# Narrow products in pairs over opposite halves of the rows, packed mixing weights, four mixture buffers and another unit order, in the recurrent block of a five-layer kernel

## What is computed

```python
xa = ln(x); sx = previous_token(xa) - xa
xxx = tanh((xa + sx * maa_x) @ maa_w1)            # 512 -> 5 x 32
xxx = einsum('blfd,fde->blfe', xxx, maa_w2)       # each 32 -> 512
xk, xw, xv, xr, xg = xa + sx * (maa_stack + xxx)
w = exp(-exp(time_decay + tanh(xw @ td_w1) @ td_w2))   # 512 -> 64 -> 512
r, k, v, g = xr @ Wr.T, xk @ Wk.T, xv @ Wv.T, silu(xg @ Wg.T)
# 32 heads of 16 x 16 state: out_t = r_t (u * k_t v_t + s), s = k_t v_t + w_t * s
x1 = x + groupnorm(out) * g @ Wo.T
x2 = x1 + sigmoid(xr2 @ Wfr.T) * (relu(xk2 @ Wfk.T) ** 2 @ Wfv.T)   # on ln(x1)
```

## Time and profile before

| what | value |
|---|---|
| median of 3 runs | 3742.41 us (3740.49 to 3743.94) |
| the profiled execution's own time | 3743.95 us |
| its span, first to last instruction | 3742.2 us |
| PE busy over the span | 3455.5 us (92%) |
| DVE, POOL, ACT busy | 2347.7, 2015.8, 1833.4 us |
| mean granted TensorE clock | 0.967 |

### The profile page before, as it was taken

The page is one execution under the profiler, slowest core; times in us unless marked ns, Lnnn a source line. Parts: engine busy times, 40 slices in busy tenths (PEclk is TensorE's granted clock), DMA queues, the critical chain, the costliest instruction groups (busy, mean ns, idle before and its releaser), DMA issues. The chain is left out here.

```text
span 3742.2 us, 59765 instructions
## 1 busy us (share of the span) xinstructions
PE 3455.5 (92%) x23516; PEld 2672.5 (71%) x23516; DVE 2347.7 (63%) x2908; ACT 1833.4 (49%) x4242; POOL 2015.8 (54%) x1079
## 2 busy tenths in 40 slices
...
GB/s 146 90 127 46 81 57 58 58 70 69 46 59 75 51 49 55 72 67 30 30 74 52 46 41 49 93 23 12 23 147 6 13 18 1 18 18 18 12 18 12
DMA packets 114303, 189.92 MB, mean 51 GB/s; under 512 B 17904, under 2 KB 36848, under 8 KB 113392
## 3 DMA queue, kind: packets, MB, share of 16 engines
...
## 5 line engine op out<-in xcount | busy, mean ns | idle before, releaser
L1025 POOL TENSOR_TENSOR l_pr<-l_pr,l_inv 128x1024 f32<-128x1024 f32 x256 | 480.0, 1895 | 382.8 <-DVE l_inv L1087 382.8
L895 ACT ACTIVATE l_pr<-l_ps_s,l_top 128x512 f32<-128x512 f32 x512 | 348.6, 690 | 352.4 <-DVE l_top L1083 271.6
L1529 POOL TENSOR_TENSOR tok_pr<-tok_pr,tok_ma 128x1024 f32<-128x1024 f32 x128 | 304.1, 2399 | 283.1 <-DVE tok_pr L1907 283.1
L2774 POOL TENSOR_TENSOR rec_rs<-rec_sE,rec_rT 128x1024 f32<-128x1024 f32 x128 | 326.8, 2555 | 215.7 <-DVE rec_sE L3262 166.7
L1020 POOL TENSOR_TENSOR l_x_lo<-ahead_piece,l_x_hi 128x1024 fp32r<-128x1024 f32 (+1 forms) x97 | 294.1, 3032 | 154.1 <-ACT l_x_hi L879 154.1
L1083 DVE TENSOR_REDUCE l_top<-l_ps_s 128x2 f32<-128x1024 f32 x256 | 304.1, 1218 | 10.5 <-PE l_ps_s L669 10.5
L3262 DVE TENSOR_TENSOR_SCAN rec_sE<-rec_wE,rec_ps_v 128x1024 f32<-128x1024 f32 x128 | 292.7, 2286 | 5.5 <-POOL rec_rs L2774 1.1
L679 PE MATMUL l_ps_t<-l_ident,l_pr 128*128 128x128 f32 x2048 | 275.2, 277 | 11.0 <-POOL l_pr L1025 4.9
L679 PEld LDWEIGHTS l_ps_t<-l_ident,l_pr 128*128 128x128 f32 x2048 | 225.6, 141 | 78.2 <-issue 60.7
L1779 ACT ACTIVATE tok_pr<-tok_pr,tok_shift 128x256 f32<-128x256 f32 x512 | 253.7, 498 | 13.4 <-DVE tok_shift L1915 12.0
L630 PE MATMUL l_ps_b<-l_x_hi,l_w_lo 128*128 128x256 f32 x784 | 226.8, 289 | 0.0
...
## 6 DMA issues: line engine op xcount, KB each, us to landing
...
```

Of the source, the lines that this page charges most:

```text
L895: act.activation(pr[t][:, h, :], ps_s[:, t % 2, h, :], ACT.Exp, bias=top[:, t, h:h + 1], accum_out=mass[:, t, h:h + 1]).then_inc(exped, 1)
L1025: pool.tensor_tensor(pr[t][:, :, :], pr[t][:, :, :], inv[:, t, :].unsqueeze(2).to_broadcast([P, 2, FEAT]), ALU.mult).then_inc(scaled, 1)
L1529: pool.tensor_tensor(tile, tile, ma[u][:, :, :].rearrange("p t k -> p (t k)").unsqueeze(1).to_broadcast([P, 2, TT * TOK]), ALU.add).then_i ...
L2774: pool.tensor_tensor(rs[j % 2][:, :, :], sE[j % 2][:, :, :], rT[s][:, :, :], ALU.mult).then_inc(rs_made, 1)
```

## The change

Four things. First, the second mixing products and the decay's second product are issued in pairs, `Mw` with `Mk`, `Mv` with `Mr`, `Mg` with `D2` (`few_rows`): each contracts over 64 rows, the one over rows 0 to 63 and the other over rows 64 to 127, into the two banks. `XX1` writes 32 and `D1` 64 output partitions. Second, the weights are packed: `m1` 256 to 160 columns, `m2` 4 to 2 blocks, `t1` 128 to 64 columns, `t2_m2b` 2 blocks to 1. Third, there are four mixture buffers for two. Fourth, all schedules but the last pass's are new, and `place` counts units in PE's own order. `lay_out` fills the packed arrays (not shown); the waits on `mixtures` and `products` are the same but for the order w, k, v, r, g in every batch.

```diff
-
-
-    FIRST_UNITS = ("T0", "T1", "XX0", "XX1", "Mw0", "Mw1", "Mk0", "Mk1", "D1", "K0", "Mv0", "Mv1", "D20", "D21", "K1",
-                   "V0", "Mr0", "Mr1", "V1", "Mg0", "Mg1", "R0", "R1", "G0", "G1", "C")
-    A_UNITS = ("T0", "T1", "XX0", "XX1", "Mw0", "Mw1", "Mk0", "Mk1", "D1", "K0", "Mr0", "Mr1", "D20", "D21", "K1",
-               "R0", "Mg0", "Mg1", "R1", "Mv0", "Mv1", "G0", "G1", "V0", "V1", "C")
+    A_UNITS = ("T0", "T1", "XX0", "XX1", "D1", "K0", "K1", "R0", "R1", "G0", "G1", "V0", "V1", "C")
+
+    PAIRS = {"Mwk": ("Mw", "Mk"), "Mvr": ("Mv", "Mr"), "Mgd": ("Mg", "D2")}
+    NARROW_UNITS = tuple(n + h for pair in PAIRS.values() for n in pair for h in "01")
     Z_UNITS = ("E", "Q", "O0", "O1", "T0", "T1", "FK0", "FK1", "FR0", "FR1", "FV0", "FV1")
-    NA, NZ = len(A_UNITS), len(Z_UNITS)
-    PROLOGUE = "LS LN T0 T1 SX XX0 XX1 Mw0 Mw1 Mk0 Mk1 D1 K0 Mv0 Mv1 D20 D21 K1 V0 Mr0 Mr1 V1"
+    NA, NZ = len(A_UNITS + NARROW_UNITS), len(Z_UNITS)
+    PROLOGUE = "LS LN T0 T1 SX XX0 XX1 Mwk0 Mw0 Mk0 Mwk1 Mw1 Mk1 D1 Mvr0 Mv0 Mr0 Mvr1 Mv1 Mr1 K0 K1 Mgd0 Mg0 D20 Mgd1 Mg1 D21 V0 V1"
     FIRST_TENSOR_SCHEDULE = (
-        "L:Mg0 L:Mg1 L:R0 L:R1", "L:G0", "L:G1 L:C", "A:T0 A:T1", "", "A:XX0 A:XX1", "A:Mw0 A:Mw1 A:Mk0 A:Mk1",
-        "A:D1 A:K0", "A:Mr0 A:Mr1 A:D20 A:D21", "A:K1 A:R0", "A:Mg0 A:Mg1 A:R1", "A:Mv0 A:Mv1 A:G0", "A:G1 A:V0",
-        "A:V1 A:C B:T0 B:T1", "B:XX0 B:XX1", "B:Mw0 B:Mw1 B:Mk0 B:Mk1")
+        "L:R0 L:R1", "A:T0 A:T1", "L:C L:G0", "A:XX0 A:XX1", "L:G1", "A:Mwk0 A:Mwk1", "A:D1 A:Mvr0", "A:K0 A:Mvr1", "A:K1",
+        "A:R0", "A:R1 A:Mgd0", "A:V0 A:Mgd1", "A:V1", "A:G0 B:T0 B:T1", "A:C A:G1 B:XX0 B:XX1", "B:Mwk0 B:Mwk1")
     TENSOR_SCHEDULE = (
-        "A:D1 A:K0", "Z:E A:Mr0 A:Mr1 A:D20 A:D21", "Z:Q A:K1", "A:R0", "A:Mg0 A:Mg1 A:R1", "A:Mv0 A:Mv1", "Z:O0 A:G0",
-        "Z:O1 A:G1", "A:V0", "A:V1 Z:T0", "Z:T1 A:C B:T0 B:T1", "Z:FK0", "Z:FK1 B:XX0 B:XX1", "Z:FR0 B:Mw0 B:Mw1 Z:FR1",
-        "B:Mk0 B:Mk1 Z:FV0", "Z:FV1")
+        "A:D1 A:Mvr0", "Z:E A:Mvr1", "Z:Q A:K0", "A:K1 A:Mgd0", "A:R0", "Z:O0 A:Mgd1", "Z:O1 A:R1", "A:V0", "A:V1",
+        "A:G0 Z:T0 Z:T1", "A:C B:T0 B:T1 A:G1", "Z:FK0", "Z:FK1 B:XX0 B:XX1", "Z:FR0 B:Mwk0", "Z:FR1 B:Mwk1 Z:FV0",
+        "Z:FV1")
     FIRST_SCALAR_SCHEDULE = (
-        "L:Mg0 L:Mg1 L:R0 L:R1", "L:G0", "A:LN L:G1", "A:T0 A:T1", "", "A:XX0 A:XX1", "A:Mw0 A:Mw1 A:Mk0 A:Mk1",
-        "A:D1 A:K0", "A:Mr0 A:Mr1 A:D20 A:D21", "A:K1 A:R0", "A:Mg0 A:Mg1 A:R1", "A:Mv0 A:Mv1 A:G0", "B:LN A:G1 A:V0",
-        "A:V1 B:T0 B:T1", "B:XX0 B:XX1", "B:Mw0 B:Mw1 B:Mk0 B:Mk1")
+        "L:R0 L:R1", "A:LN A:T0 A:T1", "L:G0", "A:XX0 A:XX1", "L:G1", "A:Mw0 A:Mk0 A:Mw1 A:Mk1", "A:D1 A:Mv0 A:Mr0",
+        "A:K0 A:Mv1 A:Mr1", "A:K1", "A:R0", "B:LN A:R1 A:Mg0 A:D20", "A:V0 A:Mg1 A:D21", "A:V1", "A:G0 B:T0 B:T1",
+        "A:G1 B:XX0 B:XX1", "B:Mw0 B:Mk0 B:Mw1 B:Mk1")
     SCALAR_SCHEDULE = (
-        "A:D1 A:K0", "Z:E A:Mr0 A:Mr1 A:D20 A:D21", "Z:Q A:K1", "B:LN A:R0", "A:Mg0 A:Mg1 Z:N2 A:R1", "A:Mv0 A:Mv1",
-        "Z:O0 A:G0", "Z:O1 A:G1", "A:V0", "Z:LN A:V1 Z:T0", "Z:T1 B:T0 B:T1", "Z:FK0 Z:XA", "Z:FK1 B:XX0 B:XX1",
-        "Z:FR0 B:Mw0 B:Mw1 Z:FR1", "B:Mk0 B:Mk1", "")
+        "A:D1 A:Mv0 A:Mr0", "Z:E A:Mv1 A:Mr1", "Z:Q A:K0", "A:K1 A:Mg0 A:D20", "Z:N2 A:R0 B:LN", "Z:O0 A:Mg1 A:D21",
+        "Z:O1 A:R1", "A:V0", "A:V1", "Z:LN A:G0 Z:T0 Z:T1", "B:T0 B:T1 A:G1", "Z:XA Z:FK0", "Z:FK1 B:XX0 B:XX1",
+        "Z:FR0 B:Mw0 B:Mk0", "Z:FR1 B:Mw1 B:Mk1", "")
     FIRST_GPSIMD_SCHEDULE = (
-        "L:Mg1 L:RK", "A:LS", "", "", "A:SX", "", "A:Mw1", "A:Mk1", "", "A:Mr1", "B:LS", "A:Mg1", "A:Mv1", "A:RK", "B:SX",
+        "A:LS L:RK", "", "A:SX", "", "", "", "A:Mw1 A:Mk1", "A:Mv1", "A:Mr1", "B:LS", "", "", "A:Mg1 A:RK", "", "B:SX",
         "B:Mw1 B:Mk1")
     GPSIMD_SCHEDULE = (
-        "", "", "A:Mr1 B:LS", "Z:N1", "A:Mg1", "", "Z:O0 A:Mv1", "A:RK Z:O1", "Z:LS", "", "Z:X", "B:SX Z:XR", "", "Z:FK1",
-        "B:Mw1", "B:Mk1 Z:FV0 Z:FV1")
+        "", "", "A:Mv1", "Z:N1 A:Mr1", "B:LS", "Z:O0", "Z:O1", "A:Mg1 Z:LS", "A:RK", "", "Z:X", "B:SX Z:XR", "", "Z:FK1",
+        "", "B:Mw1 B:Mk1 Z:FV0 Z:FV1")
     FIRST_VECTOR_SCHEDULE = (
-        "L:Mg1", "A:LS", "", "L:G0 L:G1 L:C", "A:SX", "", "A:Mw1", "A:Mk1", "", "A:Mr1", "B:LS", "A:Mg1", "A:G0 A:Mv1",
-        "A:G1 A:V0", "A:V1 A:C B:SX", "B:Mw1 B:Mk1")
+        "A:LS", "", "", "A:SX L:C L:G0", "L:G1", "", "A:Mw1 A:Mk1", "A:Mv1", "A:Mr1", "B:LS", "", "", "A:V0 A:Mg1", "A:V1",
+        "A:G0 A:C A:G1 B:SX", "B:Mw1 B:Mk1")
     VECTOR_SCHEDULE = (
-        "", "Z:E", "A:Mr1 B:LS", "Z:I", "A:Mg1", "Z:N3", "A:Mv1", "A:G0", "Z:LS A:G1", "A:V0", "A:V1 A:C", "Z:X", "B:SX",
-        "", "B:Mw1", "B:Mk1 Z:FV0 Z:FV1")
+        "", "Z:E", "A:Mv1", "Z:I A:Mr1", "Z:N3 B:LS", "", "A:Mg1", "Z:LS", "A:V0 A:V1", "A:G0", "A:C Z:X", "A:G1", "B:SX",
+        "", "", "B:Mw1 B:Mk1 Z:FV0 Z:FV1")
...
-        m1, m2 = sb("m1", [P, FT, 2 * P]), sb("m2", [P, 4, FEAT])
-        t1, t2_m2b = sb("t1", [P, FT, P]), sb("t2_m2b", [P, 2, FEAT])
+        m1, m2 = sb("m1", [P, FT, P + MIX]), sb("m2", [P, 2, FEAT])
+        t1, t2_m2b = sb("t1", [P, FT, DECAY]), sb("t2_m2b", [P, FEAT])
...
-        xm = [sb(f"xm{i}", [P, FT, TOK]) for i in range(2)]
+        xm = [sb(f"xm{i}", [P, FT, TOK]) for i in range(4)]
...
+        def units_in_order():
+
+            names = [(0, n) for n in PROLOGUE.split()]
+            for b in range(LAST):
+                for stage, unit in (n.split(":") for n in " ".join(FIRST_TENSOR_SCHEDULE if b == 0 else TENSOR_SCHEDULE).split()):
+                    if stage != "Z":
+                        names.append((b + "LAB".index(stage), unit))
+            for b, unit in names:
+                if b < BATCH and unit[:3] in PAIRS:
+                    yield from ((b, n + unit[3]) for n in PAIRS[unit[:3]])
+                elif b < BATCH and unit in A_UNITS:
+                    yield b, unit
+
+        places = {unit: n for n, unit in enumerate(units_in_order())}
+
         def place(b, unit):
-
-            return b * NA + (FIRST_UNITS if b == 0 else A_UNITS).index(unit)
+            return places[b, unit] if b >= 0 else -1
...
+        def mixed_in(name):
+            return xm[{"k": 0, "w": 1, "g": 1, "v": 2, "r": 3}[name]]
+
+        def last_reader(b, name):
+
+            return {"k": (b, "XX1"), "w": (b - 1, "G1"), "g": (b, "D1"), "v": (b - 1, "V1"), "r": (b - 1, "R1")}[name]
...
+            def few_rows(b, *units):
+
+                half, ranks = int(units[0][2]), []
+                for unit in units:
+                    pe.wait_ge(keeps(b, unit), kept_by(b, unit, 1))
+                    if unit == "Mw0":
+                        pe.wait_ge(keeps(b, "XX0"), kept_by(b, "XX0"))
+                        pe.wait_ge(keeps(b, "XX1"), kept_by(b, "XX1"))
+                    elif unit == "D20":
+                        pe.wait_ge(keeps(b, "D1"), kept_by(b, "D1"))
+                    rows = slice(HALF, P) if unit[:2] in ("Mw", "Mr", "Mg") else slice(0, HALF)
+                    w2 = m2[rows, int(unit[1] in "vr"), :] if unit[:2] in ("Mw", "Mk", "Mv", "Mr") else t2_m2b[rows, :]
+                    ranks.append((unit, w2, (tdT_xx4 if unit[:2] in ("Mg", "D2") else xxT)[rows, :]))
+                for j in range(2):
+                    c = 2 * half + j
+                    for unit, w2, xx in ranks:
+                        mm = pe.matmul(bank_of(b, unit)[:, j, :], w2[:, c * P:(c + 1) * P], xx, start=True, stop=True)
+                        if j == 1:
...
+                            mm.then_inc(a_filled, 1)
+
...
+                if unit[:3] in PAIRS:
+                    few_rows(b, *(n + unit[3] for n in PAIRS[unit[:3]]))
...
                 elif unit[:2] == "XX":
                     pe.wait_ge(mixed_x, of(b, 1, 0))
+                    cols, rows = ((slice(0, P), slice(0, P)), (slice(P, P + MIX), slice(DECAY, DECAY + MIX)))[half]
                     for t in range(FT):
-                        mm = pe.matmul(ps_a[:, 0, :], m1[:, t, half * P:(half + 1) * P], xm[0][:, t, :],
-                                       start=(t == 0), stop=(t == FT - 1))
...
+                        mm = pe.matmul(ps_a[rows, 0, :], m1[:, t, cols], xm[0][:, t, :], start=(t == 0), stop=(t == FT - 1))
...
                 elif unit == "D1":
                     pe.wait_ge(mixtures, of(b, 5, 0))
                     for t in range(FT):
-                        mm = pe.matmul(ps_a[:, 0, :], t1[:, t, :], mixed_in(b, "w")[:, t, :], start=(t == 0), stop=(t == FT - 1))
...
+                        mm = pe.matmul(ps_a[0:DECAY, 0, :], t1[:, t, :], mixed_in("w")[:, t, :], start=(t == 0), stop=(t == FT - 1))
```

More of the change, by code:

```diff
@@ L2721, in a_unit @@
                 elif unit[0] == "M" and unit[2] == "1":
-                    o = mixture(b, unit[1])
+                    o = mixture(unit[1])
                     pool.wait_ge(products, of(b, 5, o))
-                    pool.tensor_tensor(mixed_in(b, unit[1])[:, :, :], mixed_in(b, unit[1])[:, :, :], xaT[:, :, 1:TOK + 1],
```

(14 more changed lines are left out.)

44 lines of the change are left out of this document (18 added, 26 removed).

## The result

The changed kernel takes 3751.13 us (median of 20 runs, 3740.74 to 3759.39), the kernel before 3739.38 us (20 runs, 3733.55 to 3744.42). The ratio is 1.0031, with a 95% interval of 1.0024 to 1.0037: slower by 11.7 us, where I had forecast 3690, and outside my range. The profiled execution took 3749.5 us, a span of 3747.7, against 3743.95 and 3742.2 before.

The account below looks back on a forecast made before the run. PE was taken to bound the kernel, at 109.25 us a steady pass. Five full passes 25, the sixth 5, prologue and first pass 22 make 52 us off 3743.95: 3692, or 3690 as a median; range 3648 to 3728.

Parts of the forecast that it names:

- Part 1: Pair units of the mixing products: 1.07 us for 1.83, saving 0.76 a unit, 4.6 us a batch.
- rival C: Pair units in few_rows: halves don't run side by side, mode changes cost 0.3 each; 3781 us, chance 0.07 with other slowdowns.
- The walk's waits: Steady pass walked through unit by unit: new PE waits at Q, R0, transposes, XX0, FV1 and others, together 11.4 us.
- the walk's sum: Steady pass: PE's work 92.9 us plus 11.4 of waits gives 104.3, 5.0 less; 25 us over five passes.
- Part 3: Four buffers and new order in steady passes: X at 1.9 for 5.36, XR beside SX costs 1.5, FK0 no wait.
- Part 4: Prologue and first pass: 14 pair units 10.6, the load 2.0, idle time won 10; 22 us, bounds 8 and 38.
- 10 of 43 idle us as won: First pass: Mg moves out, so T0 T1, XX and D1 of batch 1 come earlier; 10 us of PE's idle saved.
- D: No change: what is saved on PE is waited for elsewhere, first pass's chains unmoved; 3736 to 3745 us, chance 0.09.
- A: PE alone bounds, so the walk's waits don't arise since the engines run ahead; 3637 us, chance 0.17.
- B: Waits move: FK0 waits again and two banks are held; 1.5 us a pass left, 3723 us, chance 0.17.

Follow-up runs that it names:

- experiment 2: Changed kernel with GpSimd's X and SX differences and VectorE's SX one step earlier and GpSimd's XR one step later: 3736.07 us, ratio 0.9988.
- experiment 1: Changed kernel with idle transposes ahead of two waits, 18 at R0 and 30 at XX0, to keep PE at work: 3729.94 us, ratio 0.9980.
- the last run of experiment 5: Changed kernel in its own order, with idle transposes ahead of all its long waits, first pass included: 3728.07 us, ratio 0.9963.
- Experiment 5: Changed kernel with r mixed before v, SX, X, XR moved, feed-forward rows normalised a step earlier, and idle transposes ahead of the waits left: 3710.20 us, ratio 0.9920.
- experiment 9: The 3710 us kernel (reordered, with idle transposes), with w's mixture of batch 1 at step 5 instead of 6 on VectorE and GpSimd: 3708.82 us, ratio 0.9923.
- experiment 8: Kernel before's order with packed weights, four buffers and pairs where two units stand together: 3772.96 us; with two placings corrected 3769.10 us.

## Why the prediction was wrong

**What held.** Part 1: the pair units take 1.06 us for 1.83; rival C is excluded in the form that I gave it. `X` takes 1.67 (I had 1.9) and `FK0` doesn't wait. The load of the packed weights: `XX0` of batch 0 no longer waits its 2.0 us. The walk's waits in a steady pass: those in the timeline from 3178.53 to 3290.35 sum to 11.7 us, and I had 11.4; that is luck in part, as below. They lie a little differently: `Q` 1.40 for 1.35, `R0` 2.38 for 1.6, the two transposes 1.69 and 1.11 for 1.9 and 1.3, `XX0` 3.92 for 2.2, and less in `FV1` and `T1` of B.

**The step that failed: the walk's sum, "PE's work in a pass is then 109.25 - 10.2 (idle) - 1.85 (clock)".** I took the clock's 1.85 us out with `FK0`'s wait, listed eight new waits, and put no clock behind any of them. Measured, at half clock against full clock: `R0` 4.96 for 3.37 (1.6 us), `XX0` and `XX1` 6.53 for 3.77 (2.8), and the stretch from `T1` of Z to `G1` 4.86 for 3.19 with its waits taken out (1.7; the full-clock figure is from the kernel of experiment 2). That is 6.0 us of longer work in the steady pass shown. What it is worth in time is less, since part of it only shortens waits: the same order at a clock of 1.00 has a pass of 107.3, so 4.5 of the 7.5 us between 104.3 and 111.8 are the clock's, nearly all of it at `R0` and `XX0` (experiment 1).

The other 3.0 us are the walk's own. At full clock the waits of this order sum to 13.6 us a pass, with the idle transposes counted as waiting (3182.70 to 3290.00 in the last run of experiment 5), where I had 11.4; in after some of them were shortened by the slow work ahead of them, and the near agreement of 11.7 with 11.4 comes from that. And PE's work is 93.8 for 92.9: `XX` takes 3.77 for 3.37 with its narrow second product, `FR0` and `FR1` 7.0 for 6.6, and the rest I can't place. The kernel before at full clock has 97.1 of work and 10.2 of waits, 107.3 as well. So the new order gave back in waits (3.4 us) what it had taken from PE's work (3.3). Experiment 5's order has 9.6 us of waits and 94.5 of work: its 104.1 shows what fewer waits are worth, and says nothing for my walk.

The clue was in the kernel before: one 7.15 us pause cost 1.85 us, and in its first pass `R0` waits only 2.21 us and its 16 matmuls then take 5.03 (2903.51 to 2908.54):

```profile
2903.51 5.38 PE L2800 MATMUL rec_ps_a<-rec_xm,rec_w_r 128*128 128x256 f32 x16 [2.21 <-POOL rec_xm L2724]
2908.54 0.82 PE L2903 MATMUL rec_ps_v<-rec_vs,rec_sel 128*128 128x512 f32 x2
```

**Part 3, contention.** I put `XR` beside `SX` at 1.5 us. It costs 4.0 (5.65 for 1.65), since GpSimd's row product follows at once and stops a second one of the four operations. The Trainium skill (SBUF — State Buffer, "SBUF: two separate sides") says that the port pair VectorE and GpSimd share is an exclusive lock, held for a whole instruction, also where the VectorE operation has two SBUF inputs and the GpSimd operation reads SBUF. The trace agrees: `SX`'s first two operations take 2.38 and 2.56 us, each until 0.28 us after a GpSimd operation ends, and the last two 0.48.

**Part 4, 22 us for the prologue and the first pass.** It came to nothing. `E` starts 2.3 us earlier (2969.4 for 2971.7), but the block had begun 2.9 earlier: from there on the stretch is 0.6 longer. In the prologue a pair follows a pair, and each second one waits 1.7 us for ScalarE, which takes back more than the 0.76 that it saved; from the block's start to the first scan it takes 61.2 us for 59.1. Two lines of PE's timeline there:

```profile
2784.35 1.13 PE L2836 MATMUL rec_ps_a<-rec_xxT,rec_m 64*128 64x256 f32 x8 [1.71 <-ACT rec_xm L3050]
2790.95 3.64 PE L2862 MATMUL rec_ps_a<-rec_xm,rec_t 128*64 128x256 f32 x8 [5.47 <-POOL rec_xm L2733]
```

In the first pass `D1` of batch 1 stands a step earlier, but starts 52.4 us behind the first scan where it started 52.3 behind it, after 8.69 us of waiting for GpSimd. Fillers there gave 2 to 3.5 us, and what an earlier mixture gives isn't clear (experiment 9). My "10 of 43 idle us as won" had no chain behind it; moving a unit up on PE moves nothing if what it reads stays. What else held these 22 us I haven't tried. The sixth pass gained 3.3 us where I had 5, and the last pass with `finish`, which I had at 0, takes 2.0 more (122.1 for 120.1); that I haven't followed up.

**The rivals.** The outcome lies nearest to D (3736 to 3745), 6 us beyond it, with A and B excluded. D's mechanism, that what is saved on PE is waited for elsewhere, is what the steady passes show at full clock (107.3 and 107.3). The clock comes on top of it, and none of my rivals had it as its mechanism, which is why slower stood at 0.07. C's price of 0.3 us for a change of mode had no row behind it; experiment 8 shows 0.1 for a unit alone.
